# A Mamba block between two ternary FFNs on one core: W_in and W_out in one buffer, a ring of eight states, and two states a chunk scanned in place in PSUM

## The chip, the core and the metric

The kernel runs on one core of a Trainium2 chip. The core has five engines with a queue of instructions each: PE (TensorE, matmuls and transposes), DVE (VectorE), ACT (ScalarE), POOL (GpSimd) and SP, which here only issues DMAs. They wait for each other by semaphores. The metric is the device time of one execution in microseconds. Before the change it is 2800.23 us, the median of 3 runs (2799.28 to 2802.76).

## The reference

The input is 4 sequences of 1024 tokens of 512 numbers. Three layers are added to it in turn:

```python
x = x + 0.5 * ffn(layernorm(x), W_up, W_gate, W_down)        # 512 -> 2048 -> 512
x = x + attn(layernorm(x), ...)                              # below
x = x + 0.5 * ffn(layernorm(x), W_up, W_gate, W_down)
# ffn: hidden = silu(x @ wu.T) * (x @ wg.T); hidden @ wd.T, weights rounded to {-1,0,1} * mean|W|
# attn, E = 1024 channels, N = 16 states a channel:
r = rmsnorm(x) * norm_w
skip, x_in = r @ W_skip, r @ W_in                            # 512 -> 1024 each
x = silu(causal_conv4(x_in) + conv_b)
delta = softplus(x @ W_delta_1 @ W_delta_2 + b_delta_2)
B, C = x @ W_B, x @ W_C                                      # [token, 16] each
h = h * exp(delta * A) + (delta * x) * B                     # scan over the tokens, E x N states
y = sum_n h[:, n] * C[n]
return resid + ((y + x * W_D) * silu(skip)) @ W_out          # 1024 -> 512
```

## The kernel before

The 4096 tokens are cut into 16 chunks of 256. Weights stay in SBUF for the whole run, W_in and W_out as fp32 of 16 KB a partition each. All engines follow one written plan: a phase "fill", then "first" (chunk 0), 14 times "loop" (chunks 1 to 14), "last" (chunk 15) and "drain". A phase has 32 slots. In a loop phase three chunks are in work at once: the end of chunk i-1 (output projection OM, second FFN: U2, G2, DN2), the scan of chunk i, and the beginning of chunk i+1 (first FFN: U1, G1, DN1; projections SK, IN; DB, DT, D2). The table `LOOP_SLOTS` says which of PE's jobs stand in which slot; ("OM_1", 7, 8) is the eighth piece of the output projection of the second 128 tokens. The other engines' work on a job follows from its slot. Lists such as `UB_LATE`, `ELEM_LATE` and `Y_EARLY` say in which slots a piece of scan work comes after the slot's other work, or before it.

The scan has 32 steps a chunk (16 states for each half of the 1024 channels, 128 partitions x 4 blocks x 256 tokens a step). For each step:

- POOL writes u*B into a slot of the ring `h` (L778, 128x1024). In chunks that don't begin a sequence it adds the carried column (L784). `h` has five slots. POOL is three steps ahead of the step's PE slot: step s is written in slot s+1.
- ACT writes exp(delta*A) into two PSUM banks `abar` (L1037), four instructions, as soon as DVE has scanned the step before out of them.
- DVE scans in two instructions from `abar` and `h` into `h` (L1342), in slot s+3, and ACT saves the last column (L1043).
- For 23 of the 32 steps PE transposes the state in eight pieces into PSUM (L1553, slot s+4), and DVE multiplies it by its column of C and adds it to y in two instructions (L1364).
- For the other nine steps (`ELEM`: 3, 9, 11, 15, 17, 18, 22, 27, 31) POOL multiplies the state in `h` by a plane of C, broadcast to all partitions (L795), and issues a DMA that adds it to `xw` in SBUF (L799). Such a DMA waits until the one before it has landed (`elem_added`). Chunk 0 has nine such steps too, the last chunk six.

SP issues the loads in the order of its program. B comes in groups of two states (`bb`, two buffers, L689, 256 KB): group q is issued when POOL has made the last u*B that reads group q-2. Group 6 serves steps 12 and 13 and waits for step 9; group 10 serves steps 24 and 25. Planes of C (`cplane`, four buffers, L699, 128 KB) stand between them. What SP waits for holds up all that stands behind it.

PE's use of the weights: OM reads `w_out` (L1668) in slots 0 to 11, IN reads `w_in` (L1619) in slots 18 to 23. Before the first chunk, `w_out`'s buffer holds the rounded weights on their way to PE (`qh`).

Of the kernel before, what the change touches and what calls it, by code (L numbers as in the profile page):

```python
# [21 lines left out]
P = 128  # L22
# [4 lines left out]
CH = 256  # L27
# [29 lines left out]
def planes_of(s):  # L57
# [42 lines left out]
    ["U1_0", "G1_0", "U1_1", "G1_1"],  # L100
    ["U1_2"],
    ["G1_2", "D2_2", "U1_3"],
    ["D2_3", "G1_3", "YT_2"],
    ["YT_3", "U1_4", "G1_4"],
    ["U1_5", ("OM_0", 4, 5), "G1_5"],
    [("OM_0", 5, 7), "U1_6", "G1_6", ("OM_1", 0, 6)],
    [("OM_0", 7, 8)],
    ["U1_7", ("OM_1", 6, 7), ("DN1_0", 0, 4)],
    ["G1_7", ("DN1_0", 4, 8)],
    [("DN1_1", 0, 2), ("DN1_0", 8, 9), ("OM_1", 7, 8)],  # L110
    [("DN1_1", 2, 8), ("DN1_0", 9, 16)],
    [],
    [("SK_0", 0, 1), ("DN1_1", 8, 16), "T2_0", "T2_1"],
    [("SK_0", 1, 2)],
    [("SK_1", 0, 2), ("SK_2", 0, 1), "U2_0"],
    [("SK_2", 1, 2), ("SK_3", 0, 2), "Tp_1", "Tp_0"],
    ["G2_0", ("IN_2", 0, 2)],
    ["U2_1", ("IN_3", 0, 2)],
# [137 lines left out]
RING = 5  # L256
ACTS = 2
UB_LATE = [1, 3, 10, 13, 15, 16, 17, 22, 23, 24, 26]
ELEM_LATE = [4, 6, 13, 14, 17, 22, 23, 25, 27, 28, 29, 30, 31]
EXP_LATE = [0, 4, 7, 8, 9, 10, 11, 12, 14, 18, 19, 22, 23, 24, 27, 28, 29, 31]  # L260
Y_EARLY = [2, 4, 6, 9, 10, 11, 13, 16, 17, 19, 20, 22, 23, 24, 28]
Y_LATE = [2, 8, 9, 10, 12, 15, 16, 17, 20, 23, 26, 27, 29, 31]
XD_0 = 0
XD_1 = 9
DOWN_AT = [2, 3, 3, 4, 4, 5, 5, 6]
NEXT_LN_FILL = 19
NEXT_LN = 29
# [179 lines left out]
def macaron_kernel(nc, resid, norm_w, W_skip, W_in, conv_w, conv_b, W_delta_1, W_delta_2, b_delta_2, W_B, W_C,  # L447
# [12 lines left out]
    with ctx:  # L460
# [106 lines left out]
        times_c, elem_added = sem("times_c"), sem("elem_added")  # L567
        scanned, hT_ready = sem("scanned"), sem("hT_ready")
# [43 lines left out]

        @block.sync
        def _(sp):
# [18 lines left out]
            sp.dma_start(w_in[:, :, :], W_in.rearrange("(d p) e -> p d e", p=P)).then_inc(win_loaded, 16)  # L633
# [58 lines left out]
            def load_c(c, s):  # L692

                g, n = elems_before(c, s), state_of(s)
                need(sp, times_c, g - ELEM_PLANES + 1)
                sp.sem_inc(sp_go, 1)
                sp.wait_ge(c_stored, 16 * (c + 1))
                sp.sem_inc(sp_go, 1)
                sp.dma_start(cplane[:, g % ELEM_PLANES, :], c_dram[n:n + 1, :].rearrange("o t -> (o t)").partition_broadcast(P)  # L699
                             ).then_inc(c_loaded[g % ELEM_PLANES], 16)  # L700

            def run(ph, i):
                if ph == "fill":
                    load_x(1)
                    load_w_out()
# [29 lines left out]
        def _(pool):  # L735
# [172 lines left out]
            def run(ph, i):  # L908
# [45 lines left out]
        def _(sc):  # L954
# [293 lines left out]
        def _(ve):  # L1248
# [86 lines left out]
            def scan_of(i, s):  # L1335
# [100 lines left out]
            def run(ph, i):  # L1436
# [79 lines left out]
        def _(pe):  # L1516
# [155 lines left out]
            def job(ph, i, name, lo, hi):  # L1672
# [92 lines left out]
```

## Time and profile before

| | |
|---|---|
| runs | 2799.28, 2800.23, 2802.76 us |
| span of the profiled execution | 2796.2 us |
| median of the runs less that span | 4.0 us |
| PE / DVE / POOL / ACT busy | 2614.3 / 2447.7 / 2382.1 / 1879.0 us |
| fill, up to the first scan | 152.5 us |
| chunk 0 (phase first) | 161.3 us |
| chunks 1 to 14 (phase loop) | 2274.3 us, 162.4 us each |
| chunk 15 (phase last) | 135.0 us |
| drain, from the last scan | 73.1 us |

The stages are counted from the first scan of one chunk to the first scan of the next. The profile gives the span of its own execution and no other time of it; the 4.0 us between the span and the median of the runs lie outside the recorded instructions or between executions. Busy shares over the whole span hide that the stages have different limits: three quarters of PE's idle time lie in the fill, chunk 0, the last chunk and the drain.

### The profile page before, as it was taken

To read this page: it belongs to the slowest core of one execution; us is meant where nothing else is said; L and a number is where in the kernel's file an instruction comes from. 1 tells how busy PE (TensorE), PEld (TensorE's weight loads), DVE (VectorE), ACT (ScalarE), POOL (GpSimd) and SP (SyncE) were. 2 spreads that over 40 slices of the span, in tenths; PEclk is the share of its full clock that TensorE was granted. 3 is DMA by queue.
4 is the path that set the end of the run, shared out by engine and by line. 5 is a ranking of instruction groups with operands and counts; after the bars stand their busy time and mean duration, and the time that the engine had idled before them with its cause. 6 is when DMAs were issued, how large, how long until landed. Compare 5 with 4: busy or idle time off the path is not lost.

```text
span 2796.2 us, 51718 instructions
## 1 busy us (share of the span) xinstructions
PE 2614.3 (93%) x17439; PEld 2021.6 (72%) x17439; DVE 2447.7 (88%) x3221; ACT 1879.0 (67%) x4340; POOL 2382.1 (85%) x2023
## 2 busy tenths in 40 slices
PE   5776899999999999999999999999999999999878
PEld 4555677777878777786777778677777877776655
DVE  4378899999999999899999999899999999999892
ACT  7374867676676767667676766767676676767651
POOL 1168899999898999999998999999999898999881
PEclk9898999999999999999999999999999999999989
DMA  7013222223222322222232222222222222222220
GB/s 274 31 55 72 60 61 76 56 58 83 59 74 60 80 50 65 77 63 73 58 81 53 70 69 63 73 63 75 54 72 66 66 69 65 73 57 68 64 55 8
DMA packets 94446, 192.44 MB, mean 69 GB/s; under 512 B 12588, under 2 KB 32232, under 8 KB 93672
## 3 DMA queue, kind: packets, MB, share of 16 engines
q0 software_dynamic: 20304, 73.93, 13.7%
q1 hardware_dynamic: 73880, 115.21, 13.0%
q8 instruction: 141, 2.31, 0.3%
q14 instruction: 121, 0.99, 0.1%
HBM read 106.26 MB, written 8.91 MB: 41 GB/s over the span
## 4 chain that ended last, share of the span: by engine, by line
POOL 41%; PE 32%; issue 12%; DVE 7%; ACT 2%; DMA 1%; POOLq 1%; DVEq 0%; ACTq 0%
POOL h L778 22%; PE ps L1596 10%; POOL h L795 7%; PE ps L1607 6%; PE ps L1619 6%; POOL hl L884 4%; PE ps L1553 4%; PE ps L1668 4%; DVE h L1342 3%; POOL u L892 2%; POOL delta L849 2%; DVE xc L1400 1%; PE ps L1629 1%; POOL h L784 1%; POOL xw L799 1%
## 5 line engine op out<-in xcount | busy, mean ns | idle before, releaser
L778 POOL TENSOR_TENSOR h<-u,bb 128x1024 f32<-128x1024 f32 x512 | 1257.8, 2466 | 27.2 <-DVE u L1417 14.2
L1342 DVE TENSOR_TENSOR_SCAN h<-ps,h 128x512 f32<-128x512 f32 x1024 | 1191.8, 1207 | 36.5 <-POOL h L784 18.6
L1037 ACT ACTIVATE ps<-delta,a_neg 128x255 f32<-128x255 f32 x2048 | 873.1, 468 | 377.0 <-DVE h L1342 374.8
L1596 PE MATMUL ps<-xh,q_up 128*128 128x256 f16 x2048 | 466.5, 275 | 36.1 <-DVE xl L1280 19.1
L1364 DVE SCALAR_TENSOR_TENSOR y<-ps,ccur,y 128x512 f32<-128x512 f32 x678 | 471.4, 738 | 6.9 <-PE ps L1553 6.3
L1596 PE MATMUL ps<-xh,q_gate 128*128 128x256 f16 x2048 | 462.7, 273 | 8.1 <-DVE xw L1433 7.8
L1596 PE MATMUL ps<-xl,q_up 128*128 128x256 f16 x2048 | 466.5, 275 | 0.0
L1596 PE MATMUL ps<-xl,q_gate 128*128 128x256 f16 x2048 | 462.4, 273 | 0.0
L1553 PE MATMUL ps<-ident,h 128*128 128x128 f32 x2968 | 398.2, 277 | 50.2 <-DVE y L1364 46.7
L1553 PEld LDWEIGHTS ps<-ident,h 128*128 128x128 f32 x2968 | 344.6, 142 | 112.7 <-issue 50.9
L884 POOL TENSOR_TENSOR hl<-act,hh 128x512 f16<-128x512 f32 x256 | 314.5, 1229 | 97.3 <-ACT hh L1064 94.4
L1607 PE MATMUL ps<-q_down,hh 128*128 128x512 fp8e4 x1024 | 388.6, 379 | 2.5 <-POOL hl L884 1.2
L1607 PE MATMUL ps<-q_down,hl 128*128 128x512 fp8e4 x1024 | 388.5, 379 | 0.0
L795 POOL TENSOR_TENSOR h<-h,cplane 128x1024 f32<-128x1024 f32 x141 | 334.8, 2374 | 0.0
L1059 ACT ACTIVATE act<-ps,tanh_sc 128x512 f32<-128x512 f32 x256 | 174.9, 683 | 201.1 <-PE ps L1596 129.0
L1372 DVE SCALAR_TENSOR_TENSOR act<-act,ps 128x512 f32<-128x512 f32 x256 | 173.6, 678 | 98.3 <-ACT act L1059 97.9
L1596 PEld LDWEIGHTS ps<-xh,q_up 128*128 128x128 fp8e4 x2048 | 201.6, 98 | 76.8 <-issue 51.8
L1619 PE MATMUL ps<-xrT,w_in 128*128 128x256 f32 x1024 | 235.3, 384 | 13.5 <-DVE xc L1400 11.2
L1668 PE MATMUL ps<-w_out,gz 128*128 128x512 f32 x512 | 243.5, 609 | 2.3 <-POOL gz L906 2.2
L1596 PEld LDWEIGHTS ps<-xh,q_gate 128*128 128x128 fp8e4 x2048 | 200.9, 98 | 39.8 <-issue 15.0
L1619 PE MATMUL ps<-xrT,w_skip 128*128 128x256 f32 x1024 | 229.5, 379 | 0.0
L1596 PEld LDWEIGHTS ps<-xl,q_up 128*128 128x128 fp8e4 x2048 | 201.6, 98 | 33.5 <-issue 4.6
(126 smaller groups left out, 3642.9 us busy)
## 6 DMA issues: line engine op xcount, KB each, us to landing
xw<-h POOLq DMA_DIRECT2D x141, 512.0 KB, 4.5
bb<-b_scratch SPq DMA_DIRECT2D x224, 256.0 KB, 3.1
cplane<-c_scratch SPq DMA_DIRECT2D x141, 128.0 KB, 3.1
xs<-in_L_attn_resid_dram SPq DMA_DIRECT2D x17, 512.0 KB, 3.5
out_dram<-xs SPq DMA_DIRECT2D x15, 512.0 KB, 4.3
wraw<-in_L_ffn_W_up_dram SPq DMA_DIRECT2D x4, 1024.0 KB, 9.6
wraw<-in_L_ffn_W_gate_dram SPq DMA_DIRECT2D x4, 1024.0 KB, 12.3
wraw<-in_L_ffn_W_down_dram SPq DMA_DIRECT2D x4, 1024.0 KB, 14.1
```

The costliest lines, as they stand in the source:

```text
L778: ins = pl.tensor_tensor(hs, u[:, :, :], bb[:, q % 2, s % PLANES:s % PLANES + 1, :].broadcast_to([P, HE, CH]), ALU.mult)
L795: pl.tensor_tensor(hs, hs, cplane[:, k:k + 1, :].broadcast_to([P, HE, CH]), ALU.mult).then_inc(times_c, 1)
L884: pl.tensor_tensor(hl[:, 2 * p:2 * p + 2, :], act[:, p % ACTS, :].rearrange("q (f t) -> q f t", f=2), hh[:, 2 * p:2 * p + 2, :], ALU.subtr ...
L1037: ins = ac.activation(abar[r][:, e, 1:], delta[:, k, 1:], ACT.Exp, scale=a_neg[:, k, n:n + 1])
L1059: ac.activation(act[:, p % ACTS, :], pp, ACT.Tanh, scale=tanh_sc[:, 0:1]).then_inc(tanh_ready, 1)
L1342: v.tensor_tensor_scan(hr, abar[r].rearrange("p e t -> p (e t)"), hr, 0.0, ALU.mult, ALU.add).then_inc(scanned, 1)
L1364: ins = v.scalar_tensor_tensor(out=yy, in0=hT[:, t, :], scalar=cc, in1=yy, op0=ALU.mult, op1=ALU.add)
L1553: ins = te.transpose(hT[:, t, e * P:(e + 1) * P], h[:, (STEPS * i + s) % RING, e, t * P:(t + 1) * P], ident[:, :])
L1596: ins = te.matmul(pp[:, f * CH:(f + 1) * CH], w[:, d, col:col + P], part[:, d, :], start=(d == 0 and part is xh), stop=(d == DB - 1 and pa ...
L1607: ins = te.matmul(pp, part[:, f, t * P:(t + 1) * P], q_down[:, f, :], start=(f == 0 and part is hh), stop=(f == FB - 1 and part is hl))
L1619: ins = te.matmul(pp[:, e * CH:(e + 1) * CH], w[:, d, col:col + P], xrT[:, d, :], start=(d == 0), stop=(d == DB - 1))
L1668: ins = te.matmul(pp, gz[:, e, t * P:(t + 1) * P], w_out[:, e, :], start=(e == 0), stop=(e == EB - 1))
```

## The change

1. `w_in` and `w_out` become two views of one buffer `w_io`. SP loads W_in into it once a loop phase, when both OM jobs are done, and W_out once a phase, when IN_3 and IN_1 are done. The loads stand in SP's program before group 6 (`W_IN_AT = 6`) and before group 10 of B. PE waits for the load ahead of IN_2 and of OM. That makes 15 loads of each in place of one. In the fill W_in is loaded when the rounded weights have left the buffer.
2. The 16 KB freed pay for a ring of eight states in place of five.
3. The steps by the C plane are 10 of 32 in place of 9 (chunk 0: 10, last chunk: 5). Of these, steps 24 and 26 of a loop chunk (11, 25 and 27 of chunk 0; 26 and 30 of the last) are "banked": DVE scans in place in PSUM, then DVE and not POOL multiplies `abar` by the C plane into `h`, in two instructions; ACT saves the last columns in two copies and sets the first columns of `abar` back to zero; POOL only issues the DMA.
4. For the steps in `ADD_NEXT` (of the loop's: 9, 18 and 26) the DMA is issued one slot later, behind the next u*B.
5. A new plan: jobs of `LOOP_SLOTS` move by a slot or two, and the lists of early and late work differ.

```diff
-    [("DN1_1", 0, 2), ("DN1_0", 8, 9), ("OM_1", 7, 8)],      # slot 11
+    [("DN1_0", 8, 9), ("OM_1", 7, 8)],
...
-RING = 5
+RING = 8
+W_IN_AT, W_OUT_AT = 6, 10
-ELEM = [3, 9, 11, 15, 17, 18, 22, 27, 31]
+ELEM = [3, 9, 10, 15, 17, 18, 22, 24, 26, 31]
-ELEM_LAST = [5, 9, 11, 17, 23, 28]
+ELEM_LAST = [5, 9, 17, 26, 30]
+BANKED = [7, 11, 16, 19, 20, 23, 24, 25, 26, 27, 28, 29, 30]
+ADD_NEXT = [1, 2, 6, 8, 9, 11, 12, 18, 21, 23, 25, 26, 30]
...
-        w_in = sb("w_in", [P, DB, E])
-        w_out = sb("w_out", [P, EB, D])
+        w_io = sb("w_io", [P, DB * E])
+        w_in = w_io[:, :].rearrange("p (d e) -> p d e", d=DB)
+        w_out = w_io[:, :].rearrange("p (e d) -> p e d", e=EB)
...
+            def load_w_in(ph, i):                            # SP
+                if ph == "fill":
+                    sp.wait_ge(q_saved, ALL_SAVED)
+                else:
+                    for t in range(TB):
+                        bk, before = job_no(ph, i, f"OM_{t}")
+                        sp.wait_ge(bank_ready[bk], before + 1)
+                sp.dma_start(w_in, W_in.rearrange("(d p) e -> p d e", p=P)).then_inc(win_loaded, 16)
+            def load_w_out(ph, i):
+                for q in (3, 1):
+                    bk, before = job_no(ph, i, f"IN_{q}")
+                    sp.wait_ge(bank_ready[bk], before + 1)
+                sp.dma_start(w_out, W_out.rearrange("(e p) d -> p e d", p=P)).then_inc(wout_loaded, 16)
...
                     for q in range(2, LOADS + 1):
+                        if q == W_IN_AT and ph == "loop":
+                            load_w_in(ph, i)
+                        if q == W_OUT_AT and "IN_1" in PHASES[ph]:
+                            load_w_out(ph, i)
                         for s in loads_of_c(i, q):
                             load_c(i, s)
                         if q < LOADS:
                             load_planes(i, q)
...
+                if out_of_bank:                              # ACT, exps of the step behind a banked one
+                    save_banked_carry(*before)
                 for r in range(2):
-                    need(sc, scanned, 2 * S - 1 + r)
+                    if out_of_bank:
+                        need(sc, banked_times_c, 2 * banked_before(*before) + r + 1)
+                        ac.activation(abar[r][:, :, 0], ident[:, 0:2], ACT.Copy, scale=0.0)
+                    else:
+                        need(sc, scanned, 2 * S - 1 + r)
...
-                    v.tensor_tensor_scan(hr, abar[r].rearrange("p e t -> p (e t)"), hr, 0.0, ALU.mult, ALU.add).then_inc(scanned, 1)
+                    v.tensor_tensor_scan(ar if is_banked(i, s) else hr, ar, hr, 0.0, ALU.mult, ALU.add).then_inc(scanned, 1)
+            def banked_state_times_c(i, s):                  # DVE, right behind the scan
+                for r in range(2):
+                    need(ve, banked_carry, 2 * banked_before(i, s) + r + 1)
+                    v.tensor_tensor(h[:, S % RING, 2 * r:2 * r + 2, :], abar[r],
+                                    cplane[:, k:k + 1, :].broadcast_to([P, 2, CH]), ALU.mult).then_inc(banked_times_c, 1)
```

How the instructions stand. First SP's queue in a loop phase, from the load of the next chunk's tokens on; before:

```order
L714 DMA xs<-in_L_attn_resid_dram 128x2x512
L699 DMA cplane<-c_scratch 128x256
L689 DMA bb<-b_scratch 128x512
L699 DMA cplane<-c_scratch 128x256
L689 DMA bb<-b_scratch 128x512
L699 DMA cplane<-c_scratch 128x256
L689 DMA bb<-b_scratch 128x512 x2
L699 DMA cplane<-c_scratch 128x256
L689 DMA bb<-b_scratch 128x512
```

The first single `bb` row is group 2, the x2 row groups 4 and 5, and the last row group 6. And now:

```order
L762 DMA xs<-in_L_attn_resid_dram 128x2x512
L747 DMA cplane<-c_scratch 128x256
L737 DMA bb<-b_scratch 128x512
L747 DMA cplane<-c_scratch 128x256
L737 DMA bb<-b_scratch 128x512
L747 DMA cplane<-c_scratch 128x256
L737 DMA bb<-b_scratch 128x512 x2
L682 DMA w_io<-in_L_attn_W_in_dram 128x4x1024
L747 DMA cplane<-c_scratch 128x256
L737 DMA bb<-b_scratch 128x512
```

The load of W_in stands between groups 5 and 6 of B. Second, POOL's queue in a loop phase from the product of step 22 on; before:

```order
L795 TENSOR_TENSOR h<-h,cplane 128x1024
L799 DMA xw<-h 128x1024
L884 TENSOR_TENSOR hl<-act,hh 128x512
L778 TENSOR_TENSOR h<-u,bb 128x1024 x3
L884 TENSOR_TENSOR hl<-act,hh 128x512
L778 TENSOR_TENSOR h<-u,bb 128x1024
L884 TENSOR_TENSOR hl<-act,hh 128x512
```

And now, where L830 is the u*B, L851 the product, L862 the adding DMA and L947 the `hl` of the FFN:

```order
L851 TENSOR_TENSOR h<-h,cplane 128x1024
L862 DMA xw<-h 128x1024
L947 TENSOR_TENSOR hl<-act,hh 128x512
L830 TENSOR_TENSOR h<-u,bb 128x1024 x2
L862 DMA xw<-h 128x1024
L947 TENSOR_TENSOR hl<-act,hh 128x512
L830 TENSOR_TENSOR h<-u,bb 128x1024
```

The second L862 is that of the banked step 24, with no product of POOL's ahead of it. Third, DVE's queue behind the next-to-last banked step of a chunk, now (L1430 the scan, L1443 the product, L1466 the y sum, L1474 and L1482 the FFN):

```order
L1430 SCALAR_TENSOR_TENSOR h<-ps,h 128x512 x2
L1466 SCALAR_TENSOR_TENSOR y<-ps,ccur,y 128x512 x2
L1474 SCALAR_TENSOR_TENSOR act<-act,ps 128x512
L1430 SCALAR_TENSOR_TENSOR ps<-ps,h 128x512 x2
L1443 TENSOR_TENSOR h<-ps,cplane 128x512 x2
L1482 SCALAR_TENSOR_TENSOR act<-ps,act 128x512
```

A banked step puts two products behind its two scans, in the same bank that ACT has to fill for the next scan.

## Rows read from the trace of the kernel before

**Rows 1.** The windows of all 14 loop chunks, the last chunk, and chunk 7.
```profile
core 0: us, PE busy (x) PEld busy (x) DVE busy (x) ACT busy (x) POOL busy (x), PEclk, DMA share, GB/s
...
313.80:2588.10 2274.30, 2231.72 (x14983) 1729.51 (x14982) 2101.68 (x2767) 1596.21 (x3751) 2094.84 (x1775) 1.00 0.27 67
2588.10:2723.10 135.00, 106.30 (x636) 78.29 (x634) 124.41 (x147) 81.24 (x200) 121.88 (x96) 0.90 0.23 59
...
1290.20:1452.40 162.20, 159.79 (x1078) 124.05 (x1077) 150.15 (x200) 114.06 (x266) 150.35 (x131) 1.00 0.28 67
```

**Rows 2.** Waits in chunk 7: total us, times, longest.
```profile
PE ps L1619 <- DVE xc L1400: 1.0, 1, 1.0
...
POOL gz L906 <- DVE xw L1433: 1.8, 2, 1.3
...
DVE xw L1433 <- DMA xw<-h: 0.5, 1, 0.5
```

**Rows 3.** Groups by line: busy us, mean ns of one, idle time before them.
```profile
L1342 DVE TENSOR_TENSOR_SCAN h<-ps,h 128x512 f32<-128x512 f32 x1024 | 1191.8, 1207 | 36.5 <-POOL h L784 18.6 <-ACT ps L1037 8.9 <-POOL h L778 7.6
L1364 DVE SCALAR_TENSOR_TENSOR y<-ps,ccur,y 128x512 f32<-128x512 f32 x678 | 471.4, 738 | 6.9 <-PE ps L1553 6.3
L1553 PE MATMUL ps<-ident,h 128*128 128x128 f32 x2968 | 398.2, 277 | 50.2 <-DVE y L1364 46.7 <-DVE y L1361 3.3
L795 POOL TENSOR_TENSOR h<-h,cplane 128x1024 f32<-128x1024 f32 x141 | 334.8, 2374 | 0.0
L1433 DVE TENSOR_TENSOR xw<-ps,xw 128x512 f32<-128x512 f32 x64 | 43.5, 682 | 5.5 <-DMA xw<-h 4.7 <-PE ps L1659 0.8
```

**Rows 4.** DMA issues: count, KB each, us from issue to landing.
```profile
bb<-b_scratch SPq DMA_DIRECT2D x224, 256.0 KB, 3.1
xs<-in_L_attn_resid_dram SPq DMA_DIRECT2D x17, 512.0 KB, 3.5
w_skip<-in_L_attn_W_skip_dram SPq DMA_DIRECT2D x1, 2048.0 KB, 8.5
w_out<-in_L_attn_W_out_dram SPq DMA_DIRECT2D x1, 2048.0 KB, 9.7
w_d<-in_L_attn_W_delta_dram SPq DMA_DIRECT2D x1, 512.0 KB, 4.5
```

**Rows 5.** SP's issues in the fill and in chunk 7, by start.
```profile
42.87 1.24 SPq L637 DMA_DIRECT2D w_d<-in_L_attn_W_delta_dram  x1
44.16 0.43 SPq L638 DMA_DIRECT2D w_skip<-in_L_attn_W_skip_dram  x1
...
1331.95 0.32 SPq L689 DMA_DIRECT2D bb<-b_scratch  x1
```

**Rows 6.** PE's last OM piece and its wait at IN_1, chunk 7.
```profile
1333.07 1.02 PE L1668 MATMUL ps<-w_out,gz 128*128 128x512 f32 x2
...
1387.55 3.72 PE L1619 MATMUL ps<-xrT,w_in 128*128 128x256 f32 x16 [0.98 <-DVE xc L1400]
```

**Rows 7.** POOL in chunk 7: u*B of steps 12, 13, 14, 24; product and DMA of step 9.
```profile
1339.82 2.36 POOL L778 TENSOR_TENSOR h<-u,bb 128x1024 f32<-128x1024 f32 x1
1342.46 2.36 POOL L795 TENSOR_TENSOR h<-h,cplane 128x1024 f32<-128x1024 f32 x1
1345.39 0.93 POOL L799 DMA_DIRECT2D xw<-h  x1 [0.57 <-POOL h L795]
1346.04 2.69 POOL L778 TENSOR_TENSOR h<-u,bb 128x1024 f32<-128x1024 f32 x1
...
1355.95 2.68 POOL L778 TENSOR_TENSOR h<-u,bb 128x1024 f32<-128x1024 f32 x1
...
1407.15 2.36 POOL L778 TENSOR_TENSOR h<-u,bb 128x1024 f32<-128x1024 f32 x1
```

**Rows 8.** DVE in chunk 7: the scans of steps 12 and 14.
```profile
1349.15 2.33 DVE L1342 TENSOR_TENSOR_SCAN h<-ps,h 128x512 f32<-128x512 f32 x2
...
1358.96 2.34 DVE L1342 TENSOR_TENSOR_SCAN h<-ps,h 128x512 f32<-128x512 f32 x2
```

More of the change, by code:

```diff
@@ L99 @@
     ["T1_1", "T1_0", ("OM_0", 0, 4)],
[L100 to L103, printed above, removed]
+    ["U1_0", "G1_0", "U1_1"],
+    ["G1_1", "U1_2"],
+    ["G1_2", "D2_2"],
+    ["U1_3", "D2_3", "G1_3", "YT_2"],
     ["YT_3", "U1_4", "G1_4"],
[L105 to L109, printed above, removed]
[L110 to L118 removed]
+    [("OM_0", 4, 6), "U1_5", "G1_5"],
+    ["U1_6", ("OM_1", 0, 5), "G1_6"],
+    [],
+    [("OM_0", 6, 8), ("OM_1", 5, 6), "U1_7", ("OM_1", 6, 7), ("DN1_1", 0, 2)],
+    ["G1_7", ("DN1_0", 0, 8)],
+    [("DN1_0", 8, 9), ("OM_1", 7, 8)],
+    [("DN1_1", 2, 8), ("DN1_0", 9, 10), ("SK_0", 0, 1)],
+    [("DN1_0", 10, 16), ("DN1_1", 8, 16)],
+    ["T2_1", "T2_0", ("SK_0", 1, 2)],
+    [],
+    [("SK_1", 0, 2), ("SK_2", 0, 1), "U2_0", ("SK_2", 1, 2)],
+    [("SK_3", 0, 2), "Tp_0", "Tp_1"],
+    ["G2_0", ("IN_2", 0, 1)],
+    [("IN_2", 1, 2), "U2_1", ("IN_3", 0, 2)],
     ["YT_0", "G2_1", ("IN_0", 0, 2)],
@@ L348, in is_elem, with is_banked, banked_before, elem_at @@
     return s in elem_of(c)
+def is_banked(c, s):
+    return s in BANKED and is_elem(c, s)
+def banked_before(c, s):
+    whole = [sum(k in BANKED for k in elem_of(j)) for j in range(c)]
+    return sum(whole) + sum(k in BANKED and k < s for k in elem_of(c))
+def elem_at(g):
+    c = 0
+    while g >= len(elem_of(c)):
+        g, c = g - len(elem_of(c)), c + 1
+    return c, elem_of(c)[g]
 def elems_before(c, s):
@@ L915, in run @@
                         u_times_b(*coming)
+                    before = step_of(ph, i, s - 1)
+                    if before and is_elem(*before) and before[1] in ADD_NEXT:
+                        add_state(*before)
                     if done and is_elem(*done) and s not in ELEM_LATE:
@@ L1038, in exps, with save_banked_carry @@
                     ins.then_inc(abar_ready, 1)
+            def save_banked_carry(i, s):
+                for r in range(2):
+                    need(sc, scanned, 2 * (STEPS * i + s) + r + 1)
+                    ac.activation(carry[:, s // N, 2 * r:2 * r + 2, state_of(s)], abar[r][:, :, CH - 1],
+                                  ACT.Copy).then_inc(banked_carry, 1)
+                need(sc, banked_carry, 2 * banked_before(i, s) + 2)
+                sc.sem_inc(carry_saved, 1)
             def save_carry(i, s):
+                if is_banked(i, s):
+                    if (i, s) == (NCH - 1, STEPS - 1):
+                        save_banked_carry(i, s)
+                    return
                 need(sc, scanned, 2 * (STEPS * i + s + 1))
@@ L1445, in run @@
                         scan_of(*step)
+                        if is_banked(*step):
+                            banked_state_times_c(*step)
                     done = step_of(ph, i, s - 1)
```

74 lines of the change are left out of this document (51 added, 23 removed).

## The prediction

> **What bounds the kernel now.** I read the windows by stage first. The 14 loop chunks take 2274.3 of 2796.2 us, 162.4 us each, and PE is busy for 2231.7 of them, 159.4 a chunk; DVE and POOL are busy for about 150 each [rows 1]. PE's clock stands at full there (1.00), so a gain in the loop comes from less work on PE or from its 3.0 us of idle time a chunk. Second, the waits of chunk 7: PE idles 2.4 us of 162.2, all of it for DVE, and the longest wait is 1.0 us at the last projection for the conv [rows 1, 2]. Third, POOL in order of time. Its busy sum looks slack, but its instructions follow each other with about 0.1 us between them: behind the product at 1342.46 come the adding DMA with 0.57 us ahead of it and a u*B that takes 2.69 in place of 2.36 us [rows 7]. Its only wait of size for another engine is 1.8 us a chunk at `gz` [rows 2]. So the loop has two full engines, PE and POOL, and DVE ties them: POOL writes u*B, DVE scans it, PE waits for DVE. In the last chunk PE has slack (106.3 of 135.0 us) and DVE is the fullest with 124.4 [rows 1].
>
> **PE: 14 fewer states transposed.** Transposed steps fall from 371 to 357: one a loop chunk, one in chunk 0, one more in the last chunk. One step costs 398.2 us / 371 = 1.07 us of PE [rows 3]. In the loop this lies on the path: -1.1 us a chunk.
>
> **POOL: fewer products, more DMAs.** Products fall from 141 to 122, DMAs rise from 141 to 155. A product costs 2.37 + 0.1 us [rows 3]. A DMA costs what stands between the product's end, 1344.82, and the next u*B, 1346.04, plus the 0.3 us by which that u*B is longer: 1.5 us [rows 7]. A loop chunk has one product fewer and one DMA more: -1.0 us. Three of its DMAs come behind a u*B, which may save up to 0.57 us each, or nothing. The last chunk has three products and one DMA fewer, -8.9 us.
>
> **DVE and ACT: the banked steps.** A loop chunk loses two y additions of 0.74 us and gains four products. None is in the trace; the nearest row is `xw<-ps,xw`, PSUM with SBUF into SBUF, 0.68 us [rows 3]. That is +2.7 - 1.5 = +1.2 us a chunk, on an engine that idles 12.3 [rows 1]: hidden. The scan that writes PSUM isn't in the trace either. I take the 1207 ns of the scan into SBUF [rows 3]; the ends are a fifth less and the double, which would add 4.8 us a chunk, all within DVE's 12.3 us of idle time if the chain lets it. ACT gains about four small instructions a banked step and idles 48 us a chunk.
>
> **The ring.** POOL's chain shows next to no wait for a ring slot, so eight slots buy little by themselves: 0 to 0.5 us a chunk. I take 0.
>
> **The reloads: what they sit in front of.** PE itself has time: W_in is asked for at OM_1's end, 1334.1, and used 30 us later; W_out is asked for at 1391.3 and used in the next phase [rows 6]. What matters is SP's queue, where the load of W_in stands ahead of group 6 of B. That group feeds the u*B of step 12, at 1339.8, which is 5.7 us behind OM_1's end [rows 6, 7]. Today the group is issued at 1331.95 and lands in 3.1 us [rows 4, 5]. Afterwards it is issued behind 2 MB in the same queue. In the fill W_skip, 2 MB, was issued at 44.16 behind W_delta_2, which landed at 47.4; W_skip landed at 52.6 [rows 4, 5]. So a queue's transfers follow each other, and 2 MB take 5.3 us of pure transfer. Alone, the W_out load took 9.7 us from issue to landing [rows 4]. The lower end is 3.5 us for 512 KB [rows 4] plus three quarters of 5.3 us, 7.4. I take 8.5, the landing of W_skip, whose shape is W_in's. Ahead of it 0.3 us for the semaphore and the issue, behind it 384 KB of plane and group, 5.3 x 384/2048 = 1.0 us. So group 6 lands 9.8 us after OM_1's end (8.7 to 11.0), and u*B of step 12 is late by 9.8 - 5.7 = 4.1 us (3.0 to 5.3).
>
> The Trainium skill has another price for this load: "DMA: Bandwidth & Descriptors", section "Anatomy of one DMA", gives a fixed 2.0 us plus the bytes over 436 GB/s, for GpSimd's path, so 6.8 us by an estimate from it; the W_out row's 9.7 us is well above it. By the page step 12 would be late by 2.4 us and the sum below would come to 2791 us.
>
> **What is late next.** Step 12 has a lead of 7.0 us before its scan (1342.2 to 1349.15), but step 14 has none: POOL works without a pause from 1339.8 to its u*B at 1355.95, which with the carried column ends at 1358.9, and the scan starts at 1358.96 [rows 7, 8]. From there DVE has one wait of 0.5 us [rows 2] until PE stands at 1387.55 waiting for DVE's conv [rows 6]. PE's order up to the end of OM_1 holds the same pieces as before, so its next OM_1 end shifts with it: each chunk repeats the delay, less what slack lies on the way. That slack is 0.5 us on DVE and at most the other 1.4 us of PE's waits behind that point [rows 1, 2], with 0.2 for the earlier DMA of step 9: 0.7 to 2.1 us. I take 1.8, since the new plan can lay its jobs over small waits.
>
> **W_out's load** stands ahead of group 10, used at 1407.15, 15.9 us behind IN_1's end at 1391.3 [rows 6, 7]. 0.3 + 9.7 + 1.0 = 11.0 us: hidden with 4.9 us to spare. If an adding DMA beside it makes both slower, the spare covers half as much again.
>
> **The sum.** A loop chunk: +4.1 (late group) - 1.8 (slack) - 1.1 (PE) = +1.2 us. POOL's saving counts inside the slack, since it comes behind the stall only in part. 14 chunks: +17. Chunk 0 has no W_in load: 0. The last chunk is DVE's: it adds 1.5 us of y work and four products (2.7 us) and POOL loses 8.9, and I take -2 (DVE waits for POOL there now; +3 if DVE is all that counts, -6 if POOL is). Fill and drain: 0; in the fill the W_in load takes the place of today's W_out load. Span 2796.2 + 15 = 2811; with the 4.0 us between span and median, 2815 us. The bounds: 3.0 late and 2.1 slack give -0.2 a chunk, 2795 us; 5.3 late and 0.7 slack give +3.5, 2847 us.
>
> **Rivals.**
> - A. The group is late and it costs nothing, because PE sets the pace and POOL catches up. For it: the lead of 7.0 us before step 12 and PE's 159.4 busy us. Against it: the scan of step 14 already starts the moment POOL is done [rows 7, 8]. Then the chunk is 162.4 - 1.1, and up to 1.4 us more where the new plan covers PE's waits: -1.1 to -2.5, 14 times, and -2: 2763 to 2783, 2773 us. Faster.
> - B. The load lands at the quick end, 7.4 us or less, and all the slack is used: -0.2 x 14 - 2 = 2795 us. For it: 2 MB move in 5.3 us when the queue is warm. Against it: 9.7 us is the one load that was alone.
> - C. The banked steps hold the chain. ACT can't fill a bank for the next scan before DVE's product has read it: 1.4 us later than today, and 0.2 for the zero column, so the next scan waits if DVE has under 2.5 us of other work. Two steps at up to 1.5 us are +3 a chunk; with PE's -1.1 and the stall partly hidden behind it, +2.5: 2833 us. For it: DVE waits 8.9 us in all for `abar` already [rows 3]. Against it: behind a banked step DVE has FFN and y work of 1.4 to 2 us.
> - D. The change doesn't do what it says: no row speaks for this, the products and transposes are counted.
>
> **How the numbers follow.** Main case (the late group, +0.3 to +3.5 us a chunk) 0.48, of which a tenth ends within 0.2% of before; A 0.29; B 0.13, two parts same and one faster; C 0.10. 0.2%, 5.6 us, is about what a measurement of this kernel can tell from no change. Faster 0.33, same 0.13, slower 0.54. The predicted time is 2815 us; the main case's own range is 2800 to 2847, and with A and C inside it 8 times in 10 lie between 2772 and 2844.
>
> **What would show it.** If I am right, POOL's u*B of step 12 has an idle time of 3 to 5 us ahead of it in each loop chunk, released by the DMA of `bb`, and none in chunk 0; the load of W_in takes 7.4 to 9.7 us; the chunk is 163 to 165 us with PE's idle time up from 3.0 to over 5 us, most of it for DVE. The group of step 24 shows no wait. If the loop chunk is under 161.5 us with the POOL wait in place, rival A holds; if there is no such wait, my reading of the queue is wrong. DVE waiting over 1 us for `abar` behind steps 24 and 26 would be C. PE's transposes drop by 112, whatever the time does.

## The result, and the profile after

The changed kernel takes 2836.82 us (median of 4 runs, 2831.91 to 2837.3) against 2800.57 before in the same comparison: ratio 1.0126, 95% interval [1.0112, 1.0141]. The forecast was 2815, slower. The direction and the place are right; the time is 22 us over the forecast, and the change costs 36 us where 15 were forecast.

The profiled execution has a span of 2835.3 us, 39.1 more than before: fill +0.8, chunk 0 +0.5, the 14 loop chunks +36.3, last chunk +2.6, drain -1.1. The windows of the loop chunks, the last chunk, chunk 7, and two short ones behind PE's wait in chunk 7 (us, busy us of PE, PEld, DVE, ACT, POOL with instructions, PE clock, DMA share, GB/s):

```profile
315.10:2625.70 2310.60, 2233.20 (x14873) 1726.57 (x14871) 2110.64 (x2795) 1595.39 (x3835) 2074.73 (x1775) 0.99 0.36 95
2625.70:2763.30 137.60, 110.47 (x662) 81.45 (x660) 128.95 (x155) 81.99 (x206) 113.92 (x92) 0.90 0.22 54
1306.80:1472.40 165.60, 159.96 (x1071) 124.31 (x1069) 151.12 (x201) 114.09 (x272) 149.13 (x132) 0.99 0.35 95
1409.20:1412.60 3.40, 3.40 (x9) 2.70 (x9) 3.40 (x5) 1.45 (x4) 2.85 (x4) 0.50 0.80 154
1412.60:1430.00 17.40, 17.40 (x150) 16.11 (x150) 16.68 (x24) 11.42 (x27) 16.06 (x11) 1.00 0.61 186
```

Against [rows 1] two things stand out. PE's idle time in the loop goes from 42.6 to 77.4 us (2310.6 - 2233.2). And its busy time does not fall (2231.7, now 2233.2), although it transposes less. The fourth row gives a part of the reason: 3.4 us at a granted clock of 0.50, the lower of the two levels (1.2 GHz). How large a part is worked out below.

The queue did what the forecast says. SP's issues around the W_in load in chunk 7 (start, us, what):

```profile
1342.11 0.32 SPq L737 DMA_DIRECT2D bb<-b_scratch  x1
1350.58 0.38 SPq L682 DMA_DIRECT2D w_io<-in_L_attn_W_in_dram  x1
1351.16 0.36 SPq L747 DMA_DIRECT2D cplane<-c_scratch  x1
1351.63 0.36 SPq L737 DMA_DIRECT2D bb<-b_scratch  x1
```

And POOL at the same place (idle time before an instruction and its releaser in brackets):

```profile
1352.03 2.36 POOL L830 TENSOR_TENSOR h<-u,bb 128x1024 f32<-128x1024 f32 x1
...
1356.11 0.19 POOL L884 TENSOR_TENSOR rt<-rt 128x2 f32<-128x2 f32 x1
1360.07 2.35 POOL L830 TENSOR_TENSOR h<-u,bb 128x1024 f32<-128x1024 f32 x1 [3.76 <-DMA bb<-b_scratch]
1362.49 0.21 POOL L836 TENSOR_TENSOR h<-h,a 128x4 f32<-128x4 f32 x1
1362.68 2.37 POOL L851 TENSOR_TENSOR h<-h,cplane 128x1024 f32<-128x1024 f32 x1
1365.01 2.36 POOL L830 TENSOR_TENSOR h<-u,bb 128x1024 f32<-128x1024 f32 x1
```

Group 6 is issued behind the load, and the u*B of step 12 stands idle for 3.76 us. It starts 9.6 us behind OM_1's end, which was 5.7 us in [rows 6, 7]. Over the loop chunks that distance is 9.3 to 10.1 us.

The waits of chunk 7, by PE, then POOL, then DVE (total us, times, longest), which answer to [rows 2]:

```profile
PE ps L1723 <- DVE xc L1502: 2.4, 1, 2.4
PE ps L1657 <- DVE y L1466: 2.0, 1, 2.0
PE ps L1679 <- DVE xs L1488: 0.5, 1, 0.5
PE ps L1711 <- POOL hl L947: 0.5, 1, 0.5
...
POOL h L830 <- DMA bb<-b_scratch: 3.8, 1, 3.8
POOL gz L969 <- DVE xw L1535: 2.7, 3, 1.6
...
DVE gz L1525 <- ACT gz L1249: 4.9, 1, 4.9
DVE xw L1535 <- DMA xw<-h: 1.6, 1, 1.6
```

POOL's pause goes through DVE to PE, and comes out in two places. At the last projection PE waits 2.4 us for the conv, where it waited 1.0. And the transposes wait 2.0 us for DVE's y sum; over the whole loop that is the larger place:

```profile
PE ps L1657 <- DVE y L1466: 28.6, 25, 2.3
PE ps L1723 <- DVE xc L1502: 21.5, 14, 2.7
```

Without the late group (e1 below) the same two are 7.5 and 15.6 us. Behind the wait for the conv the projection runs slower than in [rows 6], 5.41 us for 16 matmuls in place of 3.72:

```profile
1408.07 5.41 PE L1723 MATMUL ps<-xrT,w_io 128*128 128x256 f32 x16 [2.41 <-DVE xc L1502]
```

Groups of the page that answer to [rows 3], and its DMA rows (KB each, us to landing) that answer to [rows 4]:

```profile
L830 POOL TENSOR_TENSOR h<-u,bb 128x1024 f32<-128x1024 f32 x512 | 1253.6, 2463 | 73.0 <-DMA bb<-b_scratch 51.6
L1466 DVE SCALAR_TENSOR_TENSOR y<-ps,ccur,y 128x512 f32<-128x512 f32 x650 | 450.8, 734 | 7.7 <-PE ps L1657 7.0
L1657 PE MATMUL ps<-ident,h 128*128 128x128 f32 x2856 | 388.2, 278 | 67.3 <-DVE y L1466 61.5
L851 POOL TENSOR_TENSOR h<-h,cplane 128x1024 f32<-128x1024 f32 x122 | 289.1, 2370 | 0.4 <-issue 0.3
...
bb<-b_scratch SPq DMA_DIRECT2D x224, 256.0 KB, 3.2
w_io<-in_L_attn_W_in_dram SPq DMA_DIRECT2D x15, 2048.0 KB, 8.1
w_io<-in_L_attn_W_out_dram SPq DMA_DIRECT2D x15, 2048.0 KB, 9.1
```

The new instructions, by line and form:

```profile
L1430 DVE TENSOR_TENSOR_SCAN h<-ps,h 128x512 f32<-128x512 f32 x958 | 1114.8, 1205 | 25.1 <-ACT ps L1111 12.6 <-POOL h L830 5.3 <-POOL h L836 3.7
L1430 DVE TENSOR_TENSOR_SCAN ps<-ps,h 128x512 f32<-128x512 f32 x66 | 77.2, 1215 | 4.3 <-ACT ps L1111 2.2
L1443 DVE TENSOR_TENSOR h<-ps,cplane 128x512 f32<-128x512 f32 x66 | 41.8, 675 | 0.0
```

A scan into PSUM costs the same as one into SBUF (1215 and 1205 ns), and a banked product 0.68 us.

### The profile page after: what moved, and what is told of

Same layout as the page of the kernel before. It is cut to its first block and busy times, and to the rows that moved or that the text cites. A ratio compares the mean times of both kernels' runs of the same rounds, so it can differ in the third digit from the quotient of the medians.

```text
span 2835.3 us, 51851 instructions
## 1 busy us (share of the span) xinstructions
PE 2619.9 (92%) x17327; PEld 2023.5 (71%) x17327; DVE 2461.4 (87%) x3259; ACT 1879.8 (66%) x4439; POOL 2350.5 (83%) x2018
## 5 line engine op out<-in xcount | busy, mean ns | idle before, releaser
L830 POOL TENSOR_TENSOR h<-u,bb 128x1024 f32<-128x1024 f32 x512 | 1253.6, 2463 | 73.0 <-DMA bb<-b_scratch 51.6
L1430 DVE TENSOR_TENSOR_SCAN h<-ps,h 128x512 f32<-128x512 f32 x958 | 1114.8, 1205 | 25.1 <-ACT ps L1111 12.6
L1700 PE MATMUL ps<-xh,q_up 128*128 128x256 f16 x2048 | 465.7, 274 | 15.6 <-ACT q_gate L1061 7.6
L1700 PE MATMUL ps<-xh,q_gate 128*128 128x256 f16 x2048 | 468.8, 275 | 6.8 <-DVE xw L1535 6.1
L1700 PE MATMUL ps<-xl,q_gate 128*128 128x256 f16 x2048 | 468.8, 275 | 0.0
L1466 DVE SCALAR_TENSOR_TENSOR y<-ps,ccur,y 128x512 f32<-128x512 f32 x650 | 450.8, 734 | 7.7 <-PE ps L1657 7.0
L1657 PE MATMUL ps<-ident,h 128*128 128x128 f32 x2856 | 388.2, 278 | 67.3 <-DVE y L1466 61.5
L1657 PEld LDWEIGHTS ps<-ident,h 128*128 128x128 f32 x2856 | 332.5, 143 | 129.1 <-DVE h L1430 53.6
L947 POOL TENSOR_TENSOR hl<-act,hh 128x512 f16<-128x512 f32 x256 | 319.7, 1249 | 95.6 <-ACT hh L1151 94.3
L851 POOL TENSOR_TENSOR h<-h,cplane 128x1024 f32<-128x1024 f32 x122 | 289.1, 2370 | 0.4 <-issue 0.3
L1723 PE MATMUL ps<-xrT,w_io 128*128 128x256 f32 x1024 | 246.3, 394 | 24.4 <-DVE xc L1502 22.1
L1773 PE MATMUL ps<-w_io,gz 128*128 128x512 f32 x512 | 240.7, 604 | 1.5 <-POOL gz L969 1.4
L1700 PEld LDWEIGHTS ps<-xh,q_up 128*128 128x128 fp8e4 x2048 | 201.5, 98 | 52.4 <-issue 27.5
L1474 DVE SCALAR_TENSOR_TENSOR act<-act,ps 128x512 f32<-128x512 f32 x256 | 173.0, 676 | 75.5 <-ACT act L1146 75.4
L1723 PEld LDWEIGHTS ps<-xrT,w_io 128*128 128x128 f32 x1024 | 196.9, 198 | 56.0 <-DVE xc L1502 26.4
```

Of the source, the lines that this page charges most:

```text
L830: ins = pl.tensor_tensor(hs, u[:, :, :], bb[:, q % 2, s % PLANES:s % PLANES + 1, :].broadcast_to([P, HE, CH]), ALU.mult)
L947: pl.tensor_tensor(hl[:, 2 * p:2 * p + 2, :], act[:, p % ACTS, :].rearrange("q (f t) -> q f t", f=2), hh[:, 2 * p:2 * p + 2, :], ALU.subtr ...
L1430: v.tensor_tensor_scan(ar if is_banked(i, s) else hr, ar, hr, 0.0, ALU.mult, ALU.add).then_inc(scanned, 1)
L1466: ins = v.scalar_tensor_tensor(out=yy, in0=hT[:, t, :], scalar=cc, in1=yy, op0=ALU.mult, op1=ALU.add)
L1657: ins = te.transpose(hT[:, t, e * P:(e + 1) * P], h[:, (STEPS * i + s) % RING, e, t * P:(t + 1) * P], ident[:, :])
L1700: ins = te.matmul(pp[:, f * CH:(f + 1) * CH], w[:, d, col:col + P], part[:, d, :], start=(d == 0 and part is xh), stop=(d == DB - 1 and pa ...
```

## The experiments

All are compared with the kernel before on the same chip. "Loop" is the sum over the 14 loop chunks in the profiled execution; PE's idle time there is the loop less PE busy; the last column is POOL's idle time before the u*B of step 12 in the loop.

| kernel | median us | ratio [95%] | loop | PE busy | PE idle | POOL idle, step 12 |
|---|---|---|---|---|---|---|
| before | 2800.57 | | 2274.3 | 2231.7 | 42.6 | 0 |
| changed | 2836.82 | 1.0126 [1.0112, 1.0141] | 2310.6 | 2233.2 | 77.4 | 51.6 |
| e1 W_in behind group 6 | 2790.77 | 0.9963 [0.9950, 0.9976] | 2264.4 | 2212.6 | 51.8 | 0 |
| e2 before + W_in load ahead of 6 | 2865.12 | 1.0226 [1.0211, 1.0242] | 2339.7 | 2251.2 | 88.5 | 58.8 |
| e2b the same, 1 MB | 2806.38 | 1.0020 [1.0010, 1.0030] | 2285.0 | 2236.8 | 48.2 | 10.8 |
| e3 before + both loads, 7 and 10 | 2801.08 | 1.0001 [0.9991, 1.0010] | 2274.3 | 2231.7 | 42.6 | 0 |
| e4 changed, no loads, ring 5 | 2866.85 | 1.0231 [1.0216, 1.0247] | 2333.8 | 2235.7 | 98.1 | 0 |
| e5 changed, IN_1 second in its slot | 2843.85 | 1.0153 [1.0138, 1.0168] | 2315.9 | 2235.5 | 80.4 | 49.2 |
| e7 e1 with the old plan, none banked | 2798.39 | 0.9992 [0.9983, 1.0001] | 2274.5 | 2233.0 | 41.5 | 0 |
| e8 e1, none banked | 2851.23 | 1.0177 [1.0162, 1.0192] | 2325.9 | 2232.2 | 93.7 | 0 |
| e9 e1, no DMA a step later | 2797.53 | 0.9985 [0.9976, 0.9994] | 2265.7 | 2213.3 | 52.4 | 0 |
| e10 e1 with ring 6 | 2792.12 | 0.9964 [0.9951, 0.9977] | 2264.5 | 2212.5 | 52.0 | 0 |
| e10 e1 with ring 5 | 2875.96 | 1.0268 [1.0251, 1.0285] | 2340.4 | 2235.0 | 105.4 | 0 |
| e13 e1, last chunk not banked | 2790.60 | 0.9965 [0.9951, 0.9979] | 2264.2 | 2211.8 | 52.4 | 0 |

**e1, the load behind group 6**

```diff
-W_IN_AT, W_OUT_AT = 6, 10
+W_IN_AT, W_OUT_AT = 7, 10
```

> The changed kernel with the load of W_in one place later in SP's queue, behind group 6 of B and ahead of group 7 (used 16 us after that of group 6). All else as changed. Theory Q (the late group): the 3.7 us that POOL idles ahead of step 12 go to 0, PE's idle time at IN_1 falls under 1 us, the stretches at half clock in the loop go, and with them some 50 us: the time is about 2785 us, below the kernel before. Theory P (the plan and the banked steps cost the time, the late group is absorbed): 2830 us or more. Theory T (59 MB more traffic slow everything): 2830 us or more, since the traffic stays.

It is 46 us faster than the changed kernel and 10 us faster than before. Its loop, and POOL at step 12 in chunk 7, with the 3.76 us gone (the u*B at 1336.20 is step 12):

```profile
314.00:2578.40 2264.40, 2212.59 (x14871) 1718.77 (x14869) 2111.66 (x2796) 1594.04 (x3835) 2073.91 (x1775) 1.00 0.37 97
```

```profile
1336.01 0.20 POOL L884 TENSOR_TENSOR rt<-rt 128x2 f32<-128x2 f32 x1
1336.20 2.35 POOL L830 TENSOR_TENSOR h<-u,bb 128x1024 f32<-128x1024 f32 x1
1338.63 0.21 POOL L836 TENSOR_TENSOR h<-h,a 128x4 f32<-128x4 f32 x1
```

The load still takes 8.1 us; only its place in the queue differs. So the late group costs the changed kernel 46 us: in the loop 25.6 of PE's idle time and 20.6 of PE's busy time. It also shows what all the rest of the change is worth together: -0.7 us a loop chunk.

**e2 and e2b, the load alone in the old kernel.** The old kernel keeps its buffers, lists and ring; SP also reloads W_in into W_in's own buffer ahead of group 6, when OM_0 and OM_1 are done, whole (e2) or half (e2b, `0:2` for `0:4`). PE waits for the load ahead of IN_2, as in the change.

```diff
+            def reload_w_in(ph, i):
...
+                sp.dma_start(w_in[:, 0:4, :], W_in.rearrange("(d p) e -> p d e", p=P)[:, 0:4, :]).then_inc(win_loaded, 16)
...
+                        if q == 6 and ph == "loop":
+                            reload_w_in(ph, i)
...
+                        need(pe, win_loaded, 16 * (1 + max(i, 0)))
```

> The kernel before with one thing added: W_in is loaded again into its own buffer once a loop phase, ahead of group 6 of B, when both OM jobs are done, as in the change. No sharing, five slots, old plan, nothing banked. Theory Q: POOL idles 3.5 to 4 us ahead of step 12 in each loop chunk, and the loop chunk grows by 3 to 4 us: 2840 to 2855 us. Theory P: within 0.3% of before.

> The kernel before with only half of W_in (1 MB) loaded again ahead of group 6. Theory Q (the late group): 2.6 us less transfer leave POOL idle for 1.2 to 1.6 us ahead of step 12, and the loop has no slack for it, as the full load's 64 us for 58.8 us of POOL's idle time showed: +15 to +25 us, 2816 to 2826 us. A theory with 1 to 2 us of slack a chunk says 2801 to 2806 us.

The whole load costs 65 us in the loop, and the time is 10 us above theory Q's range; Q is right in kind and too low in size. POOL's wait for `bb` in the whole run (total, times, longest):

```profile
POOL h L796 <- DMA bb<-b_scratch: 54.4, 13, 5.1
```

The half load lands in 4.8 to 5.5 us (median 5.0) against 8.0 for the whole one, 3.0 us sooner where I had reckoned with 2.6. POOL idles 0.77 us a chunk, where I had looked for 1.2 to 1.6, and in the profiled execution the chunk grows by 0.76. That execution took 2811.5 us, though, and the median of the ten is 2806.4, 4.9 us above the kernel before and under the 2816 to 2826 that I expected. So the direction is shown, and how much of so short a pause arrives is not: all of it in this execution, less in most.

**e3, both loads in the old kernel, W_in behind group 6, W_out ahead of group 10.** The same edit with 7 for 6, and a load of `w_out` at 10, for which PE waits ahead of OM.

> The kernel before with both weights loaded again into their own buffers once a loop phase, W_in behind group 6 and W_out ahead of group 10: the traffic of the change (56 MB more), with no group late at step 12. Theory Q: 2800 to 2806 us, as before. Theory T: over 2820 us.

No change, 162.4 us a loop chunk. In the old plan the traffic itself (92 in place of 67 GB/s in the loop) costs nothing, nor does the place of W_out's load.

**e4, own buffers, no loads, ring of five, new plan and banked steps**

```diff
-RING = 8
+RING = 5
...
+        w_in_own = sb("w_in", [P, DB * E])
...
-                        if q == W_IN_AT and ph == "loop":
-                            load_w_in(ph, i)
-                        if q == W_OUT_AT and "IN_1" in PHASES[ph]:
-                            load_w_out(ph, i)
```

> The changed kernel with separate buffers for W_in and W_out, no reloads, and a ring of five: what is left are ten steps by the C plane, two of them banked, and the new plan. Theory Q: no wait ahead of step 12, about 2785 us. Theory P: 2830 us or more. If it is well above the first kernel of this set, the ring of eight is worth the difference.

Both weights are loaded once, in the fill. The loads of the loop are gone and the time is 30 us above the changed kernel's. POOL waits for ring slots here, 5.5 us a chunk. So the freed memory carries something that I had put at 0.

**e10, the ring's size alone, on e1**

```diff
-RING = 8
+RING = 6
```

and the same with 5.

> The changed kernel with the W_in load behind group 6 and a ring of five states instead of eight; buffer, reloads, plan and banked steps as in the change. Theory R (under the new plan the ring of eight carries the gain: the kernel with buffers of their own, no reloads and a ring of five ran at 2866.9, 76 us above the same plan with ring of eight and reloads): POOL waits for ring slots 4 to 6 us a chunk, loop mean 166 to 167 us, 2855 to 2875 us. Theory T (those 76 us came from something else that the kernel with buffers of its own had, since reloads and the shared buffer also went there): 2788 to 2800 us, loop mean within 0.5 of 161.75. The prediction's own term (ring of eight buys 0 to 0.5 us a chunk) asks for 2791 to 2798.

> The changed kernel with the W_in load behind group 6 and a ring of six states. Theory R with a smooth dose: a third of the way back from five slots to eight, POOL waiting for slots 1 to 3 us a chunk, loop mean 163 to 165 us, 2810 to 2840 us. If one slot more is enough (the wait is for one state that PE or an adding DMA still reads): 2790 to 2800 us. Theory T: 2788 to 2800 us.

Six slots give what eight give; five cost 84 us more than six. Theory R holds for five (1 us above its range), and the dose is a step, not a slope. With five the kernel is also 9 us slower than e4, which differs by the loads and the buffers alone: with this ring the traffic is not quite free. POOL's wait for slots with five (first the whole run, then the DMA of step 26 and the u*B of step 31 of chunk 7):

```profile
POOL h L830 <- DMA xw<-h: 50.3, 33, 4.1
```

```profile
1476.21 0.93 POOL L862 DMA_DIRECT2D xw<-h  x1 [0.29 <-issue]
1481.20 2.35 POOL L830 TENSOR_TENSOR h<-u,bb 128x1024 f32<-128x1024 f32 x1 [4.06 <-DMA xw<-h]
```

In the loop u*B waits for slots mainly at three steps: 31 (49.7 us in the 14 chunks), 15 (25.6) and 23 (10.6). With five slots step 31 needs the slot of the banked step 26, whose DMA is issued only 5 us earlier, since the scan and DVE's product come first and the DMA stands one step later besides. With six the slot is that of step 25, which PE has read. Steps 15 and 23 need the slots of steps 10 and 18, whose products POOL makes; so the banked step is more than half of the ring's price and not all of it.

**e7, the buffer and the ring of eight with the old plan.** `LOOP_SLOTS`, `ELEM` and the lists are those of before, `BANKED` and `ADD_NEXT` are empty, and the loads stand at 7 and 10.

> The changed kernel with the old plan and lists, nine steps by the C plane and none banked; the shared buffer, the ring of eight and the reloads stay, that of W_in behind group 6. The ring alone: theory R (no one waited for a slot in the old plan) 2798 to 2804 us. If the ring frees the old plan too: below 2795 us.

For the old plan eight slots buy nothing (162.5 us a chunk). The forecast's 0 holds there, and not for the new plan.

**e8, e1 without banked steps**

```diff
-BANKED = [7, 11, 16, 19, 20, 23, 24, 25, 26, 27, 28, 29, 30]
+BANKED = []
```

> As the kernel with the load of W_in behind group 6 (2790.8 us), but no step is banked: POOL makes the products of all ten steps and DVE none. POOL gains two products of 2.4 us a chunk and loses nothing. Theory POOL-bound: +3 to +4.9 us a chunk, 2830 to 2860 us. Theory PE-bound: POOL's 149 busy us leave room, 2790 to 2800 us.

60 us slower than e1. POOL makes ten products a chunk and becomes the bound: PE waits for its `hl`.

```profile
PE ps L1711 <- POOL hl L947: 42.5, 15, 3.5
```

**e9, e1 with each adding DMA right behind its product** (`ADD_NEXT = []`).

> The changed kernel with the W_in load behind group 6, and with the list of adding DMAs that are moved one step later emptied: each adding DMA is issued right behind its own product again, ring of eight. Theory N (POOL's order matters: behind its product the DMA waits with POOL's queue for the product of VectorE or for the state): POOL's wait before the DMAs' issue rises by 1 to 3 us a chunk, loop mean 162.5 to 164.5 us, 2800 to 2830 us. Theory M (the move is worth little, the ring carries it): within 3 us of 2790.8.

6.8 us slower than e1, between the two theories, and hardly in the loop (+1.3 us for 14 chunks, POOL's wait before its DMAs up by 0.3 us a chunk). Chunk 0 is 4.5 us longer and the last one 1.7. So theory M holds in the loop, and the moved DMAs pay at the ends.

**e5, IN_1 behind U2_3.** Meant to take the wait away from the projection and see whether the half clock goes with it.

```diff
-    [("IN_1", 0, 2), "U2_3", "G2_3", "U2_4"],
+    ["U2_3", ("IN_1", 0, 2), "G2_3", "U2_4"],
```

> The changed kernel with one pair of PE jobs exchanged in slot 23 of the loop: U2_3 ahead of IN_1. The group is as late as before (3.7 us), but PE has 3.5 us of matmuls where it idled for 2.4 us. Theory C (the clock): the stretches at half clock in the loop, ten in the changed kernel, go with that wait, and the time falls by 10 to 20 us, to 2817 to 2827 us. Theory N (the half clock is a symptom and costs nothing, as PE waits for others anyway): 2833 to 2840 us.

Inconclusive, and 4 us above the range of either theory: U2_3 then waits for the same conv, 2.1 us, and the stretches at half clock stay, nine for ten. The edit could not have removed more than half of them in any case, since five of the ten follow the transposes' wait for DVE's y sum.

**e13, e1 with POOL's products in the last chunk**

```diff
-    return s in BANKED and is_elem(c, s)
+    return s in BANKED and c < NCH - 1 and is_elem(c, s)
...
```

> The changed kernel with the W_in load behind group 6, and in the last chunk alone no banked steps: there POOL makes the products of steps 26 and 30, and VectorE's scans stay in SBUF; chunks 0 to 14 are untouched. In the last chunk VectorE is the fullest engine (128.9 of 137.6 us in the changed kernel, 124.4 of 135.0 before). Theory V (the last chunk is 2.6 to 3.3 us longer than before because four products of 0.7 us and their waits stand on VectorE there): last chunk 134.5 to 136.0 us in place of 138.3, total 2786 to 2789 us, against 2790.8 with the banked steps. Theory W (the last chunk is longer for the new order of its jobs, or because it has fewer adding DMAs): last chunk 137.5 to 139 us or longer, total 2790 to 2794.

The last chunk falls from 138.3 to 137.0 us, between what the two theories said, and the drain rises from 72.2 to 73.7. Together, before rounding, it is 210.6 us both times, no gain. The total is W's: the banked products are not what keeps the program's end from getting shorter. What does stays open. e1, e10 with six slots and e13 are 0.35% to 0.37% faster than before and cannot be told apart.

## Why the forecast was wrong in size

The sum for a loop chunk was +4.1 (late group) - 1.8 (slack) - 1.1 (PE) = +1.2. The runs give +2.6, and the terms can be read one by one, taking e1 as the changed kernel without the late group:

| term, us a loop chunk | forecast | measured | from |
|---|---|---|---|
| late group | +4.1 | +3.7 | 51.6 / 14, POOL's idle time for `bb` |
| slack | -1.8 | -1.9 | PE's idle time rises by only (77.4 - 51.8) / 14 = 1.8 |
| PE's busy time behind its waits | none | +1.5 | PE busy, (2233.2 - 2212.6) / 14 |
| the rest of the change | -1.1 | -0.7 | e1 against before, (2264.4 - 2274.3) / 14 |
| sum | +1.2 | +2.6 | |

**The failed step** is the sentence that PE's clock stands at full in the loop, "so a gain in the loop comes from less work on PE or from its 3.0 us of idle time". It is true of the kernel before. I carried it over to a kernel in which I myself forecast over 5 us of PE's idle time, and the sum has no term for PE becoming slower behind its new waits. That term measured +1.5 us a chunk, 20.6 us in the loop.

How much of it is the clock? In the changed kernel's clock record ten stretches of 3.4 us at 0.50 lie in the loop, in e1's one. (The last 10 us of the loop are left out here and below: every kernel has one stretch there, at a wait of PE of 2.3 to 4.2 us.) Nine stretches at half clock are at most 15.4 us. What one costs can be read where the same chunk has one in one kernel and none in another: chunk 6 of e1 and of e10 with six slots, first and second row.

```profile
1123.40:1286.70 163.30, 159.50 (x1070) 124.44 (x1069) 151.10 (x202) 114.33 (x276) 150.30 (x134) 0.99 0.36 96
1124.30:1287.20 162.90, 158.50 (x1071) 123.22 (x1069) 151.06 (x202) 114.15 (x276) 150.38 (x133) 1.00 0.37 96
```

That is 1.0 us of PE's busy time; three more such pairs (chunk 2 of e9 and of e1, chunk 11 of e10 with six slots and of e1, chunk 7 of e7 and of the kernel before) give 0.9 to 1.5. Nine of them are 8 to 14 of the 20.6 us. Not all of the 20.6 can be the clock: chunk 4 has no stretch in the changed kernel, first row, nor in e1, second row, and PE is still busy for 0.8 us longer. Chunks 8 and 12 are like it, 0.7 us each.

```profile
811.40:974.90 163.50, 159.26 (x1071) 123.07 (x1069) 151.02 (x202) 113.66 (x272) 143.93 (x106) 1.00 0.37 96
800.20:961.30 161.10, 158.42 (x1071) 123.14 (x1069) 151.08 (x201) 113.59 (x272) 143.71 (x106) 1.00 0.37 95
```

What makes PE busier there at a full clock stays open.

Over all 14 profiles there are 64 stretches at 0.50 in the loop, and each begins between 0.8 us before and 1.5 us behind the end of a wait of PE of 1.7 us or more. Only about half of the waits over 1.5 us (64 of 135) are followed by one. In the kernel before there are two waits over 1.5 us and no stretch. The Trainium skill ("TensorE: Matmul & The Clock Gate", "Part 1: The HAM clock gate") says that the gate goes by how busy PE has been and is not in step with the kernel. By that rule some waits would be hit and others not; the trace agrees. That the waits cause the stretches is argued from this order in time. The one experiment for it, e5, did not separate them. That the late group brings both is shown, by e1 (one stretch left) and e2 (from none to eight).

**Late group.** Right in mechanism and place, 0.4 us too high. The load took 7.7 to 8.5 us, median 8.1, where I took 8.5. (3.5 us and three quarters of 5.3 make 7.5 and not 7.4; nothing hangs on it.) By the fit in the Trainium skill ("DMA: Bandwidth & Descriptors", "Anatomy of one DMA"), which is for GpSimd's path, I estimated 6.8 us. That would have made the result 2791 us; the row for this load on SP's queue says 8.1.

**Slack.** The 1.9 us are what PE's idle time does not take up. In chunk time far less was absorbed: POOL idled 3.7 us a chunk and the chunk grew by 3.3 (46.2 / 14), since PE's busy time grew too. The old kernel shows the same. In e2 POOL idled 58.8 us, PE's idle time rose by 45.9 and its busy time by 19.5, and the loop grew by 65.4, more than POOL idled. So the slack that I took was near right only together with the term that I left out; by itself it takes off over four times too much.

**Ring: 0 to 0.5.** Wrong as a statement on the change, harmless in the sum, since I had counted no gain for it and the kernel has its eight slots. I had read the old plan's lack of waits for slots as a property of the ring. Under the new plan five slots cost 84 us more than six.

**PE.** The transposes fell by the 112 that I named. Without the stall PE's busy time falls by 1.4 us a chunk, more than the 1.07 reckoned, but its idle time rises by 0.7 (51.8 against 42.6 us), which I did not foresee: at the last projection, for instance, PE waits 15.6 us for DVE's conv in the loop, where it waited 10.6.

**POOL, DVE, ACT.** The banked product is 0.68 us, as its nearest row said, and the scan into PSUM costs 0.01 us more than the other. DVE's added work is hidden. e8 against e1 shows that the banked steps are worth 60 us under the new plan; they were not run under the old one.

**W_out's load.** No wait before step 24 in any loop chunk, as said.

**The ends.** The last chunk was put at -2 us and drain at 0; together they are +1.5. Fill and chunk 0, put at 0, are +1.3. The 4.0 us between span and median was only 1.5 here (2836.82 - 2835.3), which gives 2.5 back. Every execution whose span is on record took 1.8 us more than that span; the rest of such a difference is how far the profiled execution lies from the median, so it should not be carried over. So: 2815 + 19.3 (loop, 36.3 against 17) + 3.5 + 1.3 - 2.5 = 2836.6.

**Rivals.** A (absorbed) fails, since the chunk is 165.0 and not under 161.5 us. B had the slack near right by the count above (2.1 against 1.9) and the load wrong: the quickest took 7.7 us, not 7.4. C ended nearest to the time, 2833 us, by a mechanism that is not there. DVE's waits for `abar` in the loop are few,

```profile
DVE h L1430 <- ACT ps L1111: 6.7, 15, 0.7
```

and they stand at steps 29, 2 and 7; behind the banked steps 24 and 26 the next scan starts without a wait in all 14 loop chunks. And removing the banked steps (e8) makes the kernel slower. A total that fits is no evidence for its story.

## What to carry to other kernels

When a big load joins a queue, ask first what stands behind it: here 2 MB cost nothing one place later in SP's program and 46 us one place earlier. When a forecast adds idle time to a full PE, price what comes behind the waits too; here each microsecond of PE's added idle time came with 0.8 us of added busy time, about half of it from matmuls at half clock. And a buffer count that shows no wait today says nothing about another plan: five slots are enough for the old plan, six for the new one, and eight bring no more.

## What the runs showed of the hardware

- On SP's queue, a 256 KB load issued 1.05 us behind a 2 MB one landed 8.2 us after its own issue, 1.2 us behind the big one; the median of all such loads is 3.2. In e1, where the next one is issued 3.3 to 5.0 us behind the big load, it needed 4.2 to 6.0 us.
- On the same queue 1 MB of W_in took 5.0 us (e2b, median) and 2 MB 8.0 (e2).
- W_out's load (same 2 MB, 2 KB rows) takes 9.1 us beside the loop's traffic, 1.0 more than W_in's with 4 KB rows. The group behind it landed in 6.6 to 11.8 us, the long times (11.1 and more) where it was issued 1.3 to 1.5 us behind the load, the short ones (up to 7.3) where 3 us.
- A scan in place in PSUM takes 1215 ns against 1205 into SBUF; copies of two columns in ACT take 0.17 us.
- A PE wait of 1.8 to 2.7 us can be followed by 3.4 us at half clock, in the middle of a loop in which PE is busy for 97% of the time.
- The same program's executions differ with it: the changed kernel took 2831.9 us at a mean granted clock of 0.974, and 2836.5 to 2837.3 at 0.970 to 0.972.
